# A macaron block on one core: the order in which its first pair of row blocks is fed and dequantised

## The chip, the cores and the metric

The kernel runs on one NeuronCore of a Trainium2 chip. TensorE (PE) multiplies matrices; VectorE (DVE), ScalarE (ACT) and GpSimd (POOL) do element-wise work; SyncE (SP) and, in part, ACT and POOL issue transfers (DMA). Each engine works through its own instructions in order and waits for semaphores that other engines raise. The metric is the time on the device in microseconds; three runs of the kernel before gave 862.83 to 864.76 us, with a median of 863.99.

## The reference

x is [2048, 512] in float32. The block is half a gated feed-forward net, attention, and the same net again:

```python
w = (qw[:, None, :] >> shifts[None, :, None] & MAXQ).reshape(-1, qweight.shape[1])
z = ((qz[:, :, None] >> shifts[None, None, :] & MAXQ) + 1).reshape(qzeros.shape[0], -1)
W = (w - z[g_idx]) * scales[g_idx]              # for gate, up [512, 1376] and down [1376, 512]
ffn(x) = (silu(x @ Wg) * (x @ Wu)) @ Wd
x = x + 0.5 * ffn(layernorm(x))
x = x + attention(layernorm(x))                 # one head of 128, two sequences of 1024 rows
x = x + 0.5 * ffn(layernorm(x))
```

The weights are 4-bit numbers, eight packed in an int32; each row k has a group g_idx[k] that names its row of scales and zeros.

## The kernel before

**Tiling.** The 2048 rows are four blocks of 512; a pair is two of them. The inner width 1376 is cut into NT = 11 tiles of 128 columns (the last has 96). Matrix products are made from a high and a low part of each operand (`hi` by ACT, `lo` by DVE or POOL), in three passes of fp32r. Pair 0 alone uses the plain products of this section; later pairs read weights that pair 0 has prepared, and have their own functions.

**Dequantising.** In pair 0 each weight tile is made on the fly. There are 33 units: of each tile i a gate unit, an up unit and a down unit (`unit(u)`, matrix u % 3 of tile u // 3 in the kernel before). A unit goes through these steps:
- SP loads the packed integers into one of six slots of `qs` (`load_units`, 4 transfers for gate and up, 1 for down);
- DVE unpacks them (`unpack`, L1687);
- PE multiplies a one-hot of the group indices with tables of scales and zeros (`scales_zeros`, L808 and L811: eight matmuls for gate and up, two for down), into bank Z and bank S;
- DVE subtracts the zeros (`wi`, L1603) and multiplies by the scales (`wf`, L1704), both in `dequantise`;
- ACT copies `wf` as the high part (`w_hi`, L1239), POOL subtracts for the low part (`w_lo`, L2082);
- for gate and up units, SP saves `wf` to memory (`save_full`, transfer `wfull`, L523).

`wf` has two buffers, so `wf` of unit u waits for `w_lo` and the save of unit u - 2. Banks Z and S are single, so the scales of unit u wait for `wf` of unit u - 1.

**What is needed ahead.** The scales are cut by POOL into three bf16 parts (`cut_scales`), the zeros unpacked by DVE (`unpack_zeros`), and both written with small transfers into the tables `tab_gu` and `tab_d` (`table`: three pieces of scales and one of zeros). The one-hot tables `oh_gu` and `oh_d` are made from the loaded indices `idx`. x is normalised (`ln_stats`, `ln_var`, POOL's `deviation`, `ln_shift`, `ln_apply`), transposed by PE (L1020) and split into halves (`rows_hi`, `rows_lo`).

**The order.** Each engine's order is written out by hand. `plain_top` goes over the 11 tiles for the first 512 rows: on PE gate product, up product, and down product of the tile before, with `scales_zeros` of later units between them. `keep_warm(n)` issues n multiplications of the identity, two instructions each (L736), whose results nobody reads. `plain_bottom` does the next 512 rows with the finished weights.

## Time and profile before

| what | us |
|---|---|
| median of three runs | 863.99 |
| profiled execution | 863.93 |
| its span, first to last instruction | 862.1 |
| PE busy | 833.4 (97%) |
| DVE busy | 478.3 (55%) |
| ACT busy | 270.8 (31%) |
| POOL busy | 242.5 (28%) |

The span is 1.8 us shorter than the profiled execution's time; the rest lies around it. "PEld" is the loading of weights into PE, which overlaps its work. A share is an average over stages with different limits, so the rows below take the stretches apart. In a row of the trace, L811 is line 811 of the kernel before, `ps` is the memory that PE writes, `wp` and `wd` hold the gate and up weights and the down weights, `hs` and `hT` the hidden rows. "[2.13 <-PE ps L811]" says that the engine was idle for 2.13 us ahead of the row, and what ended that.

### The profile page before, as it was taken

The page shows a single profiled execution, that of the slowest core. Times are in us where ns is not written, and L with a number is a line of the kernel's source. Part 1 is how long each engine was busy: PE and PEld are TensorE (multiplying, and loading weights), DVE is VectorE, ACT ScalarE, POOL GpSimd, SP SyncE. Part 2 cuts the span into 40 slices and gives each one's busy share as a digit, 9 for nine tenths or more (in the row PEclk, how much of TensorE's full clock was granted, in tenths as well). Part 3 has the DMA queues.
Part 4 walks back from the last instruction along what each step waited for, and adds up shares of the span by engine and source line. Part 5 has one row for each costly group of instructions (what it writes and reads, how often), then busy time and mean ns, then how long its engine had stood idle before and what let it go on. Part 6 is the DMA issues. An engine that isn't in the chain of part 4 may idle for free.

```text
span 862.1 us, 10734 instructions
## 1 busy us (share of the span) xinstructions
PE 833.4 (97%) x4040; PEld 678.7 (79%) x4040; DVE 478.3 (55%) x800; ACT 270.8 (31%) x465; POOL 242.5 (28%) x197
## 2 busy tenths in 40 slices
PE   4799999999999999999999899999999999999998
PEld 4567678887888888788888788888887888888786
DVE  5577763564745454454867677445435744434452
ACT  3233322353511211241574584112112511112121
POOL 5344331463210524030235344041510201101100
PEclk9999999999999999999999999999999999999999
DMA  5667747985485444242115126854444154444121
GB/s 130 189 209 228 232 172 233 322 327 193 167 324 170 132 162 124 74 159 75 73 62 186 46 94 254 338 170 131 163 116 167 50 195 160 142 162 141 46 97 50
DMA packets 72272, 139.36 MB, mean 162 GB/s; under 512 B 25549, under 2 KB 36477, under 8 KB 67229
## 3 DMA queue, kind: packets, MB, share of 16 engines
q1 hardware_dynamic: 70908, 136.91, 47.0%
q10 hardware_dynamic: 1152, 1.36, 0.6%
q8 instruction: 32, 0.52, 0.3%
q0 software_dynamic: 160, 0.42, 0.2%
q14 instruction: 20, 0.16, 0.1%
HBM read 100.54 MB, written 37.95 MB: 161 GB/s over the span
## 4 chain that ended last, share of the span: by engine, by line
PE 73%; DVE 2%; ACT 0%; issue 0%; POOL 0%; DVEq 0%; ACTq 0%; POOLq 0%
PE ps L722 36%; PE ps L729 33%; PE ps L740 2%; PE ps L1125 1%; DVE mx L1919 0%; DVE pT L1603 0%; DVE stats L1614 0%; POOL t L2082 0%; DVE oT L1603 0%; DVE t L1603 0%; ACT oT L1239 0%; DVE hT L1603 0%; PE ps L1051 0%; ACT pr L1463 0%; DVE u L1606 0%
## 5 line engine op out<-in xcount | busy, mean ns | idle before, releaser
L722 PE MATMUL ps<-blk,ring 128*128 128x512 f32 (+1 forms) x1386 | 320.9, 389 | 0.1
L722 PEld LDWEIGHTS ps<-blk,ring 128*128 128x128 f32 (+1 forms) x1386 | 256.7, 185 | 58.1 <-DVE blk L1603 0.5
L729 PE MATMUL ps<-wd,hT 128*128 128x512 f32 (+1 forms) x1056 | 250.8, 392 | 0.8 <-DVE hT L1603 0.7
L729 PEld LDWEIGHTS ps<-wd,hT 128*128 128x128 f32 (+1 forms) x1056 | 196.8, 188 | 43.5 <-DVE hT L1603 1.2
L2124 POOL TENSOR_TENSOR h<-h,u 128x512 f32<-128x512 f32 (+1 forms) x33 | 42.7, 1295 | 324.2 <-ACT h L1358 324.2
L729 PE MATMUL ps<-xT,wp 128*128 128x512 f32 x480 | 115.8, 396 | 0.9 <-POOL wp L2082 0.7
L729 PEld LDWEIGHTS ps<-xT,wp 128*128 128x128 f32 x480 | 88.4, 188 | 22.5 <-issue 2.0
L1606 DVE TENSOR_TENSOR u<-ps,p1s 128x512 f32<-128x512 f32 (+1 forms) x66 | 45.4, 687 | 97.3 <-PE ps L722 97.2
L1358 ACT ACTIVATE h<-h 128x512 f32<-128x512 f32 (+1 forms) x33 | 20.9, 632 | 176.1 <-DVE h L1606 176.1
L1606 DVE TENSOR_TENSOR u<-ps,u 128x512 f32<-128x512 f32 (+1 forms) x66 | 45.6, 691 | 25.6 <-PE ps L722 24.6
L1606 DVE TENSOR_TENSOR h<-ps,p1s 128x512 f32<-128x512 f32 (+1 forms) x33 | 22.8, 691 | 64.1 <-PE ps L722 64.1
L1603 DVE TENSOR_TENSOR hT<-h,hT 128x512 fp32r<-128x512 f32 (+1 forms) x44 | 30.7, 712 | 24.8 <-ACT hT L1239 24.8
L1353 ACT ACTIVATE g<-ps 128x512 f32<-128x512 f32 (+1 forms) x33 | 19.7, 598 | 76.0 <-PE ps L722 76.0
L1239 ACT ACTIVATE hT<-u 128x512 fp32r<-128x512 f32 (+1 forms) x33 | 20.9, 632 | 64.5 <-DVE u L1810 64.5
L1810 DVE TENSOR_TENSOR u<-u,g 128x512 f32<-128x512 f32 (+1 forms) x33 | 38.8, 1177 | 1.1
L2092 POOL TENSOR_SCALAR xn<-xn,mv,rstd 128x512 f32<-128x512 f32 x18 | 38.3, 2140 | 0.5
L1239 ACT ACTIVATE hT<-h 128x512 fp32r<-128x512 f32 (+1 forms) x44 | 27.0, 629 | 35.5 <-PE ps L729 35.5
L2082 POOL TENSOR_TENSOR wp<-wf,wp 128x512 fp32r<-128x512 f32 x20 | 26.6, 1332 | 38.2 <-ACT wp L1239 38.2
L1603 DVE TENSOR_TENSOR hT<-u,hT 128x512 fp32r<-128x512 f32 (+1 forms) x33 | 22.8, 692 | 23.0 <-ACT hT L1239 23.0
L2087 POOL TENSOR_TENSOR rstd<-rstd,mhalf 128x4 f32<-128x4 f32 x12 | 15.1, 1256 | 68.5 <-DVE rstd L1624 68.5
L1835 DVE SCALAR_TENSOR_TENSOR xres<-ps,xres 128x512 f32<-128x512 f32 x32 | 21.6, 689 | 18.5 <-PE ps L729 18.5
L1603 DVE TENSOR_TENSOR wi<-qs,ps 128x512 bf16<-128x512 int32 (+2 forms) x33 | 22.3, 676 | 16.0 <-PE ps L811 11.1
(124 smaller groups left out, 877.8 us busy)
## 6 DMA issues: line engine op xcount, KB each, us to landing
ring<-wsaved SPq DMA_DIRECT2D x29, 1024.0 KB, 5.0
ring<-wsaved SPq DMA_DIRECT2D x33, 768.0 KB, 4.3
wsaved<-wp SPq DMA_DIRECT2D x10, 1024.0 KB, 5.0
stream<-xres SPq DMA_DIRECT2D x32, 256.0 KB, 2.3
xn<-stream SPq DMA_DIRECT2D x8, 1024.0 KB, 7.4
xres<-stream SPq DMA_DIRECT2D x32, 256.0 KB, 3.8
...
```

The lines of the kernel that those rows point to most:

```text
L722: mm = pe.matmul(ps[0:w, bank, :], ring[:, slot, which, a, kt, 0:w], blk[:, which, b, kt, :], start=not onto and kt == 0 and n == 0, stop= ...
L729: mm = pe.matmul(bank_ap, lhs(a), rhs(b), start=first and n == 0, stop=last and n == 2)
L1239: return act.activation(dst, src, ACT.Copy)
L1353: act.activation(g1[0:w, n % 2, :], ps[0:w, product_bank(n // NT + 1, 0), :], ACT.Silu).then_inc(s_g1, 1)
L1358: act.activation(hidden(i)[0:width(i), :], hidden(i)[0:width(i), :], ACT.Silu).then_inc(s_g2, 1)
L1603: return dve.tensor_tensor(out=dst, in0=a, in1=b, op=ALU.subtract)
L1606: return dve.tensor_tensor(out=dst, in0=a, in1=b, op=ALU.add)
L1810: dve.tensor_tensor(out=u2[0:w, n % 2, :], in0=u2[0:w, n % 2, :], in1=g1[0:w, n % 2, :], op=ALU.mult)\
L1835: dve.scalar_tensor_tensor(out=xres[:, r, :], in0=ps[:, down_bank(q, half, r), :], scalar=0.5, in1=xres[:, r, :], op0=ALU.mult, op1=ALU.ad ...
L2082: return pool.tensor_tensor(out=dst, in0=a, in1=b, op=ALU.subtract)
L2092: pool.tensor_scalar(x_rows(t)[:, r, :], x_rows(t)[:, r, :], mv[:, t % 2, r, 0:1], rstd[:, t % 2, r:r + 1], ALU.subtract, ALU.mult).then_i ...
L2124: pool.tensor_tensor(out=hidden(i)[0:w, :], in0=hidden(i)[0:w, :], in1=u3[0:w, n % 2, :], op=ALU.mult).then_inc(s_h2, 1)
```

## The change

The change touches only the order and the placing of work in pair 0:
- **Units.** The order is now gate 0, up 0, gate 1, up 1, down 0, gate 2, up 2, down 1, and so on (`UNIT_ORDER`; `made(m, i)` is the place of a unit in it, counted from 1). A down unit is dequantised one tile later than before.
- **First transfers.** The down zeros are loaded first on ACT's queue (on POOL's before), the group table ahead of the gate and up zeros on SP's. POOL waits only for the scales before it cuts them, and issues the down indices behind that. The pieces of the gate and up tables are shared out between SP and ACT, and issued as they get ready.
- **Start.** PE has 6 `keep_warm` instead of 10 ahead of everything, the first unit's scales ahead of the transposes of x and the second's ahead of the last of them; 4 and 2 stand further down where 6, 6 and 6 stood. DVE unpacks the down zeros first, and does units 0 and 1 ahead of x's low halves; ACT does the high half of unit 0 ahead of x's. The one-hot of the down indices comes after tile 0's hidden rows.
- **Saves.** ACT issues the save `wfull` of a unit behind its own copy, in place of SP.
- **Second rows.** The statistics of the second 512 rows are split over two tiles, and ACT normalises them instead of DVE.
- In `scales_zeros` the matmuls for zeros and for scales alternate. ACT runs one small Silu early, so that it loads one table where it loaded two. Two semaphores of the attention weights become one.

```diff
@@ -331,8 +332,15 @@
             return e - 1 if e == NT + 2 else e - 2
+        UNIT_ORDER = ((0, 0), (1, 0)) + tuple(mi for i in range(1, NT) for mi in ((0, i), (1, i), (2, i - 1))) + ((2, NT - 1),)
         def unit(u):
-            return u % 3, u // 3
+            return UNIT_ORDER[u]
+        def made(m, i):
+            return UNIT_ORDER.index((m, i)) + 1
         def unit_view(u, flat):
             m, i = unit(u)
@@ -563,33 +567,35 @@
...
             for m in range(2):
                 sp.dma_start(sc_gu[:, m * SC:(m + 1) * SC], flat(scales[m], SC)).then_inc(d_cut_gu, 16)
+            sp.dma_start(grp[:, :], groups).then_inc(d_grp, 16)
             for m in range(2):
-                sp.dma_start(zq_gu[m * ZP:(m + 1) * ZP, :], flat(zeros[m], ZC)).then_inc(d_cut_gu, 16)
-            sp.dma_start(grp[:, :], groups).then_inc(d_grp, 16)
+                sp.dma_start(zq_gu[m * ZP:(m + 1) * ZP, :], flat(zeros[m], ZC)).then_inc(d_zq_gu, 16)
             sp.dma_start(idt[:, :], ident).then_inc(d_small, 16)
             sp.dma_start(shift[:, :], shifts).then_inc(d_small, 16)
             load_units([0])
-            sp.wait_ge(s_cut, CUT_STEPS)
-            sp.wait_ge(s_tab, ZERO_STEPS)
-            table(sp, 1)
-            load_units([1, 2])
+            for j in range(2):
+                sp.wait_ge(s_cut, 2 * j + 1)
+                for m in range(2):
+                    table(sp, m, pieces=(j,))
+            load_units([1])
+            load_units([2, 3])
             sp.wait_ge(s_cut, 2 * CUT_STEPS)
             sp.wait_ge(s_tab, 2 * ZERO_STEPS)
             table(sp, 2)
-            load_units([3, 4, 5])
+            load_units([4, 5])
             for u in range(UNITS):
-                save_full(u)
                 load_units([u + QSLOTS])
-                if u == 3:
+                if u == 5:
                     load_rows(1, x, ROWS)
...
@@ -792,22 +798,20 @@
...
-                for rows, bank in ((slice(row + Z_ROW, row + Z_ROW + g), Z_BANK), (slice(row, row + 3 * g), S_BANK)):
...
+                for k in range(1 if m == 2 else KT):
+                    for rows, bank in ((slice(row + Z_ROW, row + Z_ROW + g), Z_BANK), (slice(row, row + 3 * g), S_BANK)):
...
@@ -815,39 +819,38 @@
...
                     if i == 0:
                         plain_product(0, 0, 0, by_tile=True)
-                        scales_zeros(2)
-                        pe.wait_ge(s_wlo, 2)
+                        pe.wait_ge(s_wlo, made(1, 0))
                         plain_product(0, 0, 1, (0, 1))
                         scales_zeros(3)
                         plain_product(0, 0, 1, (2, 3))
-                        scales_zeros(4)
-                        keep_warm(6)
+                        keep_warm(2)
                         continue
                     if i == 1:
                         plain_product(0, i, 0, (0, 1))
-                        scales_zeros(5)
+                        scales_zeros(4)
                         plain_product(0, i, 0, (2, 3))
                     else:
                         plain_product(0, i, 0)
+                    scales_zeros(3 * i + 2)
+                    pe.wait_ge(s_wlo, made(1, i))
+                    plain_product(0, i, 1)
                     scales_zeros(3 * i + 3)
-                    pe.wait_ge(s_wlo, 3 * i + 2)
-                    plain_product(0, i, 1)
-                    scales_zeros(3 * i + 4)
                     if i < NT - 1:
-                        pe.wait_ge(s_wlo, 3 * i)
+                        pe.wait_ge(s_wlo, made(2, i - 1))
                         down(0, 0, i - 1)
-                        scales_zeros(3 * i + 5)
+                        scales_zeros(3 * i + 4)
...
@@ -1012,21 +1015,22 @@
...
             pe.wait_ge(d_small, 32)
-            keep_warm(10)
+            keep_warm(6)
+            pe.wait_ge(d_tab[0], 64)
+            pe.wait_ge(s_oh, 3)
+            scales_zeros(0)
             for r in range(RT):
+                if r == 3:
+                    pe.wait_ge(d_tab[1], 64)
+                    scales_zeros(1)
                 pe.wait_ge(s_ln[0], r + 1)
                 for k in range(KT):
                     mm = pe.transpose(ps[:, 4 + k, r * P:(r + 1) * P], xn0[:, 0, r, k * P:(k + 1) * P], idt[:, :])
                     if r == RT - 1:
                         mm.then_inc(s_turn, 1)
-            pe.wait_ge(d_tab[0], 64)
-            pe.wait_ge(s_oh, 3)
-            scales_zeros(0)
-            keep_warm(6)
-            pe.wait_ge(d_tab[1], 64)
-            scales_zeros(1)
-            keep_warm(6)
+            scales_zeros(2)
+            keep_warm(4)
...
@@ -1256,6 +1260,10 @@
...
                 act.wait_ge(s_wf, u + 1)
                 copy(unit_weights(u, 0), unit_view(u, wf[:, u % 2, :])).then_inc(s_whi, 1)
+                m, i = unit(u)
+                if m < 2:
+                    act.dma_start(unit_view(u, wfull[i, :, m, :]), unit_view(u, wf[:, u % 2, :])).then_inc(d_full[u % 2], 16)
...
@@ -1284,11 +1292,15 @@
...
-                    for u in (2, 3) if i == 0 else (3 * i + 3,):
-                        w_hi(u)
+                    w_hi(3 * i + 2)
+                    if i == 0:
+                        w_hi(3)
                     plain_hi(0, i)
+                    if i:
+                        w_hi(3 * i + 3)
                     w_hi(3 * i + 4)
-                    w_hi(3 * i + 5)
+                    if i in (7, 8):
+                        ln_apply(1, (0, 1) if i == 7 else (2, 3))
...
@@ -1425,17 +1436,24 @@
...
+            act.dma_start(cuts[1][4], flat(zeros[2], ZC_D)).then_inc(d_zq_d, 16)
             for r in range(RT):
                 act.dma_start(xn0[:, 0, r, :], x[r * P:(r + 1) * P, :]).then_inc(d_x0[r], 16)
             for m in range(2):
                 act.dma_start(idx[FOLD * m:FOLD * m + FOLD, GU_COLS], spread(g_idx[m])).then_inc(d_idx_gu, 16)
+            act.wait_ge(s_cst, 1)
+            act.activation(spare_act[:, :], mhalf[:, 0:1], ACT.Silu)
             act.wait_ge(s_cut, CUT_STEPS)
-            act.wait_ge(s_tab, ZERO_STEPS)
-            table(act, 0)
+            table(act, 0, pieces=(2,))
+            act.wait_ge(s_tab, 2 * ZERO_STEPS)
+            table(act, 0, pieces=(3,))
+            table(act, 1, pieces=(2, 3))
             ln_apply(0)
+            w_hi(0)
             rows_hi(0)
-            w_hi(0)
...
@@ -1713,28 +1731,34 @@
...
-                dequantise(1)
-                dve.wait_ge(s_ohd, 2)
-                one_hot(dve, hots, DOWN_COLS, 1, oh_d[:, :])
...
-                    for u in (2, 3, 4) if i == 0 else (3 * i + 3,):
-                        dequantise(u)
+                    if i != 1:
+                        dequantise(3 * i + 2)
+                    if i == 0:
+                        dequantise(3)
...
+                    plain_lo(0, i)
+                    if i == 0:
+                        dve.wait_ge(s_ohd, 2)
+                        one_hot(dve, hots, DOWN_COLS, 1, oh_d[:, :])
+                        dequantise(4)
+                        dequantise(5)
+                    else:
...
-                    plain_lo(0, i)
-                    dequantise(3 * i + 5)
...
@@ -1886,10 +1910,13 @@
...
-            dve.wait_ge(d_cut_gu, 64)
             tables = maker(dve, s_tab)
+            dve.wait_ge(d_zq_d, 16)
+            unpack_zeros(dve, tables, *cuts[1])
+            ln_stats(0, (0, 1))
+            dve.wait_ge(d_zq_gu, 32)
             unpack_zeros(dve, tables, *cuts[0])
-            ln_stats(0)
+            ln_stats(0, (2, 3))
...
@@ -1900,11 +1927,9 @@
...
-            dve.wait_ge(d_cut_d, 32)
-            unpack_zeros(dve, tables, *cuts[1])
-            dequantise(0, unpack_next=False)
+            dequantise(0)
+            dequantise(1)
             rows_lo(0)
-            unpack(1)
...
@@ -2138,24 +2163,24 @@
...
-            pool.dma_start(zq_d, flat(zeros[2], ZC_D)).then_inc(d_cut_d, 16)
-            for row, first in ((0, 0), (FOLD, D_FROM)):
-                pool.dma_start(idx[row:row + FOLD, DOWN_COLS], spread(g_idx[2][first:first + D_COLS])).then_inc(d_idx_d, 16)
             pool.memset(mhalf[:, :], -0.5).then_inc(s_cst, 1)
             pool.wait_ge(s_cst, 1)
             cutter = maker(pool, s_cut)
-            pool.wait_ge(d_cut_gu, 64)
+            pool.wait_ge(d_cut_gu, 32)
             cut_scales(pool, cutter, *cuts[0])
-            pool.wait_ge(d_cut_d, 32)
+            for row, first in ((0, 0), (FOLD, D_FROM)):
+                pool.dma_start(idx[row:row + FOLD, DOWN_COLS], spread(g_idx[2][first:first + D_COLS])).then_inc(d_idx_d, 16)
...
-            compare_low(pool, hots, DOWN_COLS, 1, oh_d[:, :])
             for u in range(UNITS):
-                if u == 16:
+                if u == 2:
+                    compare_low(pool, hots, DOWN_COLS, 1, oh_d[:, :])
+                if u == 19:
                     deviation(1)
...
```

PE from its first instruction on, before (L736 is `keep_warm`, L1020 the transposes of x, L811 and L808 `scales_zeros`, L729 products):

```order
L736 MATMUL ps<-idt 128x128 x10
L1020 MATMUL ps<-idt,xn_80 128x128 x16
L811 MATMUL ps<-tab_gu,oh_gu 128x128 x8
L736 MATMUL ps<-idt 128x128 x6
L811 MATMUL ps<-tab_gu,oh_gu 128x128 x8
L736 MATMUL ps<-idt 128x128 x6
L729 MATMUL ps<-xT_85,wp 128x512 x12
L808 MATMUL ps<-tab_d,oh_d 128x512 x2
L729 MATMUL ps<-xT_85,wp 128x512 x6
L811 MATMUL ps<-tab_gu,oh_gu 128x128 x8
L729 MATMUL ps<-xT_85,wp 128x512 x6
L811 MATMUL ps<-tab_gu,oh_gu 128x128 x8
```

and in the changed kernel (L742, L1029, L815 and L813, L735 in the same roles):

```order
L742 MATMUL ps<-idt 128x128 x6
L815 MATMUL ps<-tab_gu,oh_gu 128x128 x8
L1029 MATMUL ps<-idt,xn_81 128x128 x12
L815 MATMUL ps<-tab_gu,oh_gu 128x128 x8
L1029 MATMUL ps<-idt,xn_81 128x128 x4
L815 MATMUL ps<-tab_gu,oh_gu 128x128 x8
L742 MATMUL ps<-idt 128x128 x4
L735 MATMUL ps<-xT_86,wp 128x512 x18
L815 MATMUL ps<-tab_gu,oh_gu 128x128 x8
L735 MATMUL ps<-xT_86,wp 128x512 x6
L742 MATMUL ps<-idt 128x128 x2
L735 MATMUL ps<-xT_86,wp 128x512 x6
```

Unit 0's scales moved ahead of the transposes, unit 1's ahead of the last four, and the down block of two matmuls (L808) left the first up product.

DVE from the first `wi` on, before (L1603 with `wi` and L1704 are a unit, L1687 an unpacking, L448 the one-hot of the down indices):

```order
L1603 TENSOR_TENSOR wi<-qs,ps 128x512
L1704 TENSOR_TENSOR wf<-wi,ps 128x512
L1603 TENSOR_TENSOR xT_85<-ps,xT_85 128x512 x4
L1687 TENSOR_SCALAR qs<-qs,shift 128x512
L1603 TENSOR_TENSOR wi<-qs,ps 128x512
L1704 TENSOR_TENSOR wf<-wi,ps 128x512
L1687 TENSOR_SCALAR qs<-qs,shift 128x512
L448 SCALAR_TENSOR_TENSOR oh_d<-idf,grp,oh_d 128x768
L1603 TENSOR_TENSOR wi<-qs,ps 128x512
L1704 TENSOR_TENSOR wf<-wi,ps 128x512
L1687 TENSOR_SCALAR qs<-qs,shift 128x512
L1603 TENSOR_TENSOR wi<-qs,ps 128x512
```

and in the changed kernel (L1705 unpacking, L1621 and L1722 a unit, L1742 the hidden rows `hs`, L458 the one-hot), from the third unpacking on:

```order
L1705 TENSOR_SCALAR qs<-qs,shift 128x512
L1621 TENSOR_TENSOR xT_86<-ps,xT_86 128x512 x4
L1621 TENSOR_TENSOR wi<-qs,ps 128x512
L1722 TENSOR_TENSOR wf<-wi,ps 128x512
L1705 TENSOR_SCALAR qs<-qs,shift 128x512
L1621 TENSOR_TENSOR wi<-qs,ps 128x512
L1722 TENSOR_TENSOR wf<-wi,ps 128x512
L1705 TENSOR_SCALAR qs<-qs,shift 128x512
L1742 TENSOR_TENSOR hs<-hs,ps 128x512
L1621 TENSOR_TENSOR hT<-hs,hT 128x512
L458 SCALAR_TENSOR_TENSOR oh_d<-idf,grp,oh_d 128x768
L1621 TENSOR_TENSOR wi<-qs,ps 128x512
```

The low halves of x moved behind two whole units and three unpackings, and the one-hot from ahead of the third unit to behind the hidden rows of tile 0.

## Rows read from the trace of the kernel before

**Rows 1.** Waits of TensorE over the whole run: who waited for whom, us, times, longest.
```profile
PE ps L736 <- DMA shift<-in_shifts: 11.9, 1, 11.9
PE ps L811 <- DVE wf L1704: 6.1, 7, 1.8
```

**Rows 2.** Busy time of TensorE by stretch: length, busy, instructions, clock, DMA share, GB/s.
```profile
22.10:48.00 25.90, 19.62 (x111) 1.00 0.70 218
48.00:128.00 80.00, 79.13 (x433) 1.00 0.62 201
```

**Rows 3.** TensorE in order of time: start, length, engine, line, operation, [idle before].
```profile
11.92 4.38 PE L736 MATMUL ps<-idt 128*128 128x128 f32 x20 [11.92 <-DMA shift<-in_shifts]
...
17.98 0.41 PE L811 MATMUL ps<-tab_gu,oh_gu 4*128 4x128 bf16 x8
18.32 1.60 PE L736 MATMUL ps<-idt 128*128 128x128 f32 x12
...
22.09 3.02 PE L729 MATMUL ps<-xT,wp 128*128 128x512 f32 x12
...
26.68 1.65 PE L729 MATMUL ps<-xT,wp 128*128 128x512 f32 x6 [0.73 <-POOL wp L2082]
30.15 0.41 PE L811 MATMUL ps<-tab_gu,oh_gu 4*128 4x128 bf16 x8 [1.82 <-DVE wf L1704]
30.48 1.66 PE L729 MATMUL ps<-xT,wp 128*128 128x512 f32 x6
...
44.65 3.03 PE L729 MATMUL ps<-wd,hT 128*128 128x512 f32 x12
47.61 0.39 PE L808 MATMUL ps<-tab_d,oh_d 10*128 10x512 bf16 x2
47.93 3.04 PE L729 MATMUL ps<-xT,wp 128*128 128x512 f32 x12
```

**Rows 4.** DVE in order of time, first 45 us.
```profile
9.57 0.69 DVE L1614 BATCH_NORM_STATS2 stats<-xn 128x6 f32<-128x512 f32 x1 [0.39 <-DMA xn<-in_L_attn_x]
...
13.32 0.74 DVE L448 SCALAR_TENSOR_TENSOR oh_gu<-idf,grp,oh_gu 128x512 bf16<-128x512 f32 x1
...
18.54 0.69 DVE L1603 TENSOR_TENSOR wi<-qs,ps 128x512 bf16<-128x512 int32 x1 [2.13 <-PE ps L811]
19.27 0.69 DVE L1704 TENSOR_TENSOR wf<-wi,ps 128x512 f32<-128x512 bf16 x1
19.87 2.48 DVE L1603 TENSOR_TENSOR xT<-ps,xT 128x512 fp32r<-128x512 f32 x4
...
24.50 1.01 DVE L448 SCALAR_TENSOR_TENSOR oh_d<-idf,grp,oh_d 128x768 bf16<-128x768 f32 x1
...
29.41 0.69 DVE L1704 TENSOR_TENSOR wf<-wi,ps 128x512 f32<-128x512 bf16 x1 [2.63 <-DMA wfull<-wf]
...
43.57 0.69 DVE L1704 TENSOR_TENSOR wf<-wi,ps 128x512 f32<-128x512 bf16 x1 [3.20 <-DMA wfull<-wf]
```

**Rows 5.** SP's queue in order of time, the first save.
```profile
25.67 1.53 SPq L523 DMA_DIRECT2D wfull<-wf  x1
```

**Rows 6.** ACT in order of time.
```profile
17.76 2.06 ACT L1239 ACTIVATE xT<-ps 128x512 fp32r<-128x512 f32 x4 [1.40 <-PE ps L1020]
...
24.87 1.28 ACT L1286 ACT_TABLE_LOAD   x1
```

**Rows 7.** POOL in order of time.
```profile
15.45 2.22 POOL L445 TENSOR_SCALAR oh_d<-idf,grp 128x768 bf16<-128x768 f32 x1
20.76 1.28 POOL L2082 TENSOR_TENSOR wp<-wf,wp 128x512 fp32r<-128x512 f32 x1 [3.10 <-ACT wp L1239]
```

**Rows 8.** The saves `wfull` of the first 60 us: issue to landing.
```profile
DMA to landing us min/median/max: 2.3/3.2/6.1
```

**Rows 9.** TensorE's waits from 48 to 130 us, and DVE's normalising in order of time.
```profile
PE ps L811 <- DVE wf L1704: 0.9, 2, 0.7
...
96.37 2.90 DVE L1635 TENSOR_SCALAR xn<-xn,mv,rstd 128x512 f32<-128x512 f32 x4
```

70 lines of the change are left out of this document (35 added, 35 removed).

## The prediction

> **What bounds the kernel now.** I read the waits of TensorE first, then its busy time by stretch, then its rows in order of time, and last what the engines that feed it did. TensorE bounds the run: it is busy 833.4 of 862.1 us (the page's first part, quoted above). All that another order can win is in the 28.7 us that it idles, and in fillers that count as busy. The waits [rows 1] show two large entries: 11.9 us until the constants have landed, and 6.1 us in seven waits for DVE's product `wf`, a dequantised unit. By stretch [rows 2] TensorE is busy 19.62 of 25.90 us between 22.1 and 48.0, and 79.13 of the next 80.00. So the dequantising holds it up in the first two tiles and hardly later, and the stretch before 22.1 is a start in which nothing of the kernel's main work runs.
>
> The rows in order of time [rows 3] show where. Fillers run from 11.92 to 16.30, x's transposes follow, and unit 0's scales and zeros come only at 17.98. The first product (gate of tile 0) starts at 22.09, gate of tile 2 at 47.93. I use these two as marks: whatever the change does ahead of 47.93 is worth what it moves the second mark, since behind it TensorE is nearly full.
>
> DVE's rows [rows 4] say why. `wi` of unit 0 waits 2.13 us for TensorE's scales, because these stand behind the transposes. Then `wf` waits 2.63 us at 29.41 and 3.20 us at 43.57 for a save `wfull` to land: a buffer of `wf` is free only when the save of two units earlier has left it. The first save is issued by SP at 25.67 [rows 5], 5.7 us after its data was ready at 19.96, behind the loads that stand ahead of it in SP's queue. That is the main stall: `wf` is at 29.41, the next scales at 30.15.
>
> **Start, up to the first product.** x's statistics keep their time: DVE still waits for x's last rows until 9.57 [rows 4]. The down zeros move ahead of them; they took 1.9 us in all behind the one-hot, and now fit into time in which DVE waited for transfers. The index transfer, `nmr`, and the one-hot (ready at 13.32 + 0.74 = 14.06) move little, since their queue is the same; I take the same times. Fillers are 12 instead of 20 instructions; 20 took 4.38 us, so 12 end at 11.92 + 2.6 = 14.5. Unit 0's scales then run at 14.6 instead of 17.98, `wf` of unit 0 ends two DVE instructions of 0.69 later, near 16.5. Unit 1's scales follow at 16.5, its `wf` at 18.3. The unpacking of unit 2 (0.48) stands ahead of x's low halves, so these start at 18.8 (19.87 before), the first ending at 19.4.
>
> ACT gives the high half of unit 0 first (0.63) and then issues a save (0.6), so x's high halves start at 17.8, as before [rows 6]. POOL's low half of unit 0 (1.28 [rows 7]) ends at 18.4, not 22.04. TensorE has unit 2's scales and 8 filler instructions (12 took 1.60 us, so 1.07) from 18.35 and reaches the first product at 19.8. Bounds: 18.4, when POOL is ready and x too, and 22.09, where nothing is gained. I take 19.8: a gain of 2.3.
>
> **From the first product to gate of tile 2.** A product that is followed by a scales block lasts 2.96 us (44.65 to 47.61), a block 0.32 (47.61 to 47.93), a half product 1.6 (1.66 at 30.48, whose end overlaps what follows) [rows 3]. In the new order stand: gate 0 2.7 (nothing of another kind behind it), half 1.6, block 0.33, half 1.6, four filler instructions 0.53, half 1.6, block 0.33, half 1.6, block 0.33, up 2.96, block 0.33, down 2.96, block 0.33: 17.2 us. One wait stays. Unit 4, the first down unit, needs the one-hot of the down indices, which now stands behind tile 0's hidden rows on DVE. Up of tile 0 ends at 26.1; unpacking and `hs` end at 27.4, the ACT copy with a save ahead of it at 28.1, the low half at 28.8, the one-hot (1.01 at 24.50 [rows 4]) at 29.8. TensorE is there at 28.2 and waits about 1.5 us. Its bounds are 0 and 3, the latter if POOL's comparison (2.22 [rows 7]), which also moves between its unit copies, holds unit 2 up. So gate of tile 2 starts at 19.8 + 17.2 + 1.5 = 38.5. Before it was 47.93. One block of 0.33 has then still to be done which was done before, as the down units are now made one tile later. The gain is 47.93 - 38.5 - 0.33 = 9.1, the 2.3 of the start included.
>
> The save stalls go for this reason: ACT issues a save right behind its own copy, at about 17.2 for unit 0, and the median landing is 3.2 us [rows 8], so the buffer is free at 20.4, ahead of `wf` of unit 2 at 22. Of unit 2's and 3's saves, the same. What is late next is the chain of the down one-hot above.
>
> **Behind the mark.** Two waits of together 0.9 us for `wf` between 48 and 130 [rows 9] stood behind the statistics and x's normalising on DVE (2.90 us at 96.37 [rows 9]). That normalising goes to ACT, in two parts, and the statistics are split: I take 0.8 as gained, bounds 0 and 0.9. What covers the new ACT work: ACT is busy a third of this part (five activations of 0.6 for a tile) and gets two issues of 0.6 per tile and four activations of 0.7 once. The 22 blocks for gate and up now alternate between two rows of banks: a down block of as many columns, which alternates, takes 0.32 to the next product, a gate block 0.33 (30.15 to 30.48 [rows 3]); that is 20 x 0.01 to 0.02 = 0.3 at most, and the same as a loss if the switches cost. I take 0.1. The one table load for ACT moves ahead; the second (1.28 at 24.87 [rows 6]) lay under a wait for up of tile 0 and is worth nothing. Joining the two semaphores of the attention weights, behind a wait for pair 1's end, costs nothing.
>
> **Sum.** 9.1 + 0.8 + 0.1 = 10.0 against the profiled execution's 863.93 us (span 862.1 and 1.8 around it), which is 0.06 under the median of 863.99. That gives 854.0.
>
> **Rivals.**
> 1. *The start isn't gained, 856.0.* Index and x land later since the down zeros are issued ahead of them on ACT, and x's low halves stand behind three DVE instructions more. Of that, 20 against 12 fillers speak for a gain; against it, that x's last rows and the indices bound the start in [rows 4]. First product at 22: 2.2 less gained, 856.2 with the first unpacking late as well.
> 2. *The clock is low at the first product, 856.5.* The fillers before show both levels: 20 instructions in 4.38 us at first, 12 in 1.60 later [rows 3], that is 0.22 against 0.13 each, the 1.2 and 2.4 GHz levels, the rise coming while TensorE ran without a break from 11.92. Now there are fewer fillers, and gaps between the transposes. A first product at the lower level takes 1.6 to 2 times 3.02 us, so 1.8 to 3.0 more; I take 2.5. Against it: the idle stretch of 2 us before 30.15 did not lower the rate (six matmuls in 1.66 us behind it). The Trainium skill ("TensorE: Matmul & The Clock Gate", Part 1) says that the array runs at half rate until it has been busy for some time and falls back after idling; by this rule a thinned start could begin its main work slow. The trace has the slow start, but no fall.
> 3. *Slower: the saves set the pace, 867.5.* A save now starts a copy and an issue behind `wf`, 1.3 us. Its longest landing was 6.1 us [rows 8], at the time of x's second load. If that were the rule, `wf` of a unit would come 1.3 + 6.1 + 0.7 = 8.1 us behind that of two units earlier, where TensorE's pace for two units is 6.56. 1.5 us lost for each of nine tiles is 13.5, less the 10.0: 3.5 slower. It decides from a landing of 4.6 us on. The median of 3.2 speaks against it, and that the save no longer queues behind loads on SP. The Trainium skill ("DMA: Bandwidth & Descriptors", Queues, rings and completion order) says that each transfer engine takes the queues in turn, so that ACT's queue gets its share beside SP's; by this rule landings get shorter than 3.2. No row of before shows a save on ACT's queue.
> 4. *A shorter lead, 858.* The down units have lost a tile of lead. From a block to the low half it takes 0.41 + 0.69 + 0.69 + 0.63 + 1.29 = 3.7 us of the 6.56 that each unit now has. Were an ACT issue and a wait added to each, some tiles would wait 0.5: nine of them cost 4.
>
> **How the numbers follow.** My forecast has a chance of 0.62, own range 852 to 856. Rival 1 has 0.12, rival 2 0.12, rival 3 0.04, rival 4 0.07; 0.03 is left for a gain under 852. The range of 8 in 10 reaches from 851.8 to 857.6. A change of 0.2% (1.7 us) is what a measurement of this kernel can tell from none: faster 0.95, same 0.01, slower 0.04.
>
> **What would show it.** Right: the first product near 19.8; no wait of DVE's `wf` for a `wfull` landing; one wait of TensorE before the first down block at about 28, of 1 to 2 us, for the one-hot; gate of tile 2 near 38.5; no wait of TensorE in the nine tiles behind it. Wrong: a first product at 22 or one that takes over 4 us; saves that land over 4.6 us late again and again; waits of TensorE for `wf` or POOL's low halves in the steady tiles; or the time lost again in the later pairs, where nothing should change.

## The result and the profile after

| kernel | median us | lowest to highest | runs | ratio to before, 95% interval |
|---|---|---|---|---|
| before | 863.79 | 862.83 to 865.65 | 6 | |
| changed | 860.35 | 859.46 to 861.33 | 6 | 0.9960 [0.9948, 0.9972] |

The change is worth 3.4 us by the medians; forecast were 10.0, and 860.35 lies above the range's upper end of 857.6. The profiled execution of the changed kernel took 859.65 us, its span 857.8, so 4.3 us less than before, and the rest of this section accounts for these 4.3.

TensorE's waits (engine, line waited for, us in total, times, longest) answer to [rows 1]:

```profile
PE ps L742 <- DMA shift<-in_shifts: 7.9, 1, 7.9
PE ps L815 <- DMA tab_gu<-parts_gu: 4.0, 1, 4.0
PE ps L735 <- DVE v L1621: 3.7, 1, 3.7
PE ps L813 <- DVE oh_d L458: 1.7, 1, 1.7
...
PE ps L815 <- DVE wf L1722: 0.7, 1, 0.7
```

The seven waits for `wf` (6.1 us) are down to one of 0.7. A new one has come, 4.0 us for the table transfer `tab_gu`, and one of 1.7 for the down one-hot `oh_d`. The constants land 4 us earlier (7.9 against 11.9), the cause of which no run here takes apart, and which only lengthens the wait for the tables. In order of time (start, length, engine, line, operation, [idle before]), against [rows 3]:

```profile
7.95 2.93 PE L742 MATMUL ps<-idt 128*128 128x128 f32 x12 [7.95 <-DMA shift<-in_shifts]
14.90 0.61 PE L815 MATMUL ps<-tab_gu,oh_gu 4*128 4x128 bf16 x8 [4.03 <-DMA tab_gu<-parts_gu]
15.44 2.82 PE L1029 MATMUL ps<-idt,xn 128*128 128x128 f32 x12
...
21.62 4.36 PE L735 MATMUL ps<-xT,wp 128*128 128x512 f32 x18
...
31.39 0.39 PE L813 MATMUL ps<-tab_d,oh_d 10*128 10x512 bf16 x2 [1.66 <-DVE oh_d L458]
31.71 1.79 PE L735 MATMUL ps<-xT,wp 128*128 128x512 f32 x6
33.44 0.60 PE L815 MATMUL ps<-tab_gu,oh_gu 4*128 4x128 bf16 x8
33.97 4.19 PE L735 MATMUL ps<-xT,wp 128*128 128x512 f32 x12
...
41.68 3.06 PE L735 MATMUL ps<-xT,wp 128*128 128x512 f32 x12
```

x's transposes (L1029) take 0.23 us each here and took 0.12 before (16 of them from 16.14 to 17.98), so TensorE ran at its lower rate. The granted clock's rows show 1.00 there all the same, so in the start the rate is read off the matmuls. The first product starts at 21.62 (22.09 before), gate of tile 2 at 41.68 (47.93 before). Up of tile 1, at 33.97, takes 4.19 us where every other product of 12 matmuls in this stretch takes 3.0 to 3.1. The stretches show why (stretch, its length, PE busy, PEld, DVE, ACT, POOL, then TensorE's granted clock, DMA share, GB/s):

```profile
30.00:32.00 2.00, 0.60 (x3) 0.38 (x4) 1.41 (x3) 0.00 (x0) 0.00 (x0) 1.00 0.74 222
32.00:34.00 2.00, 2.00 (x15) 1.13 (x14) 1.70 (x3) 0.64 (x2) 0.00 (x0) 0.77 0.40 104
34.00:36.00 2.00, 2.00 (x7) 1.61 (x6) 1.77 (x3) 0.88 (x2) 1.28 (x1) 0.50 0.62 215
36.00:38.00 2.00, 2.00 (x9) 1.42 (x7) 0.00 (x0) 0.23 (x1) 1.29 (x1) 0.88 1.00 300
48.00:128.00 80.00, 80.00 (x436) 56.70 (x435) 56.29 (x100) 27.79 (x45) 33.70 (x26) 1.00 0.62 201
```

After the wait for the one-hot the granted clock fell to 0.50 (1.2 of 2.4 GHz) and was whole again before 38. From 48 on TensorE is busy all the time (79.13 of 80.00 before, [rows 2]).

Of the stall that the change was after, DVE's product `wf` waiting for a save, this is left of before's two waits of 2.63 and 3.20 us [rows 4]:

```profile
47.02 0.69 DVE L1722 TENSOR_TENSOR wf<-wi,ps 128x512 f32<-128x512 bf16 x1 [1.16 <-DMA wfull<-wf]
```

Over the whole run `DVE wf` waited for saves 7.0 us in 4 waits before, and 1.2 us in 1 after. ACT issues the first save as it starts its own copy, where SP issued it at 25.67 [rows 5], behind nine loads whose issuing had kept it from 19.89 on:

```profile
17.07 0.34 ACTq L1266 DMA_DIRECT2D wfull<-wf  x1
```

**Where the lead went.** The lead of the changed kernel over before, at the same instruction in both traces: 0.5 us at the first product, 6.25 at gate of tile 2, 6.3 at the start of pair 1 (229.49 against 235.81), 5.9 before pair 1's attention product (484.27 against 490.14), 5.0 at pair 2 (514.09 against 519.10), 5.0 at DVE's last instruction (853.85 against 858.86), 4.3 at the end of the span. The chain of waits (start, us, what) of before:

```profile
387.85 24.58 PE ps L729 x108
...
415.64 1.75 PE ps L740 x16
...
490.14 4.63 PE ps L729 x24
```

and of after:

```profile
381.56 21.84 PE ps L735 x96
...
404.90 4.51 DVE xn L1653 x4
409.46 1.97 PE ps L746 x16
...
484.27 5.49 PE ps L735 x24
```

The first loss, 0.45 us, is DVE's normalising of the attention's rows: its four instructions take 4.58 us after and 4.14 before, and they now end the chain, where TensorE's own products did. Why they take longer no run takes apart. The second, 0.86 us, is the same product in 5.49 us instead of 4.63. It stands in both kernels behind a wait of 3.6 us for `v`, and in both the clock falls behind that wait: where a later product of the same size takes 3.04 us, this one loses 1.6 us before and 2.5 after. The rows of before:

```profile
490.14 4.63 PE L729 MATMUL ps<-pT,v 128*128 128x256 f32 x24 [3.64 <-DVE v L1603]
...
502.87 3.04 PE L729 MATMUL ps<-pT,v 128*128 128x256 f32 x24
```

The granted clock of before is 1.00 from 480 to 490 and 0.83 from 490 to 500; that of after is 0.68 from 480 to 490, a stretch that holds the product from 484.27 on, and 0.98 from 490 to 500.

### The profile page after: what moved, and what is told of

Same layout as the page of the kernel before. It is cut to its first block, busy times and chain, and to the rows that moved or that the text cites. A ratio compares the mean times of both kernels' runs of the same rounds, so it can differ in the third digit from the quotient of the medians.

```text
span 857.8 us, 10671 instructions
## 1 busy us (share of the span) xinstructions
PE 833.5 (97%) x4008; PEld 678.0 (79%) x4008; DVE 477.0 (56%) x797; ACT 272.6 (32%) x469; POOL 240.9 (28%) x196
## 4 chain that ended last, share of the span: by engine, by line
PE 73%; DVE 3%; ACT 1%; issue 0%; POOL 0%; DVEq 0%; ACTq 0%; POOLq 0%
PE ps L728 37%; PE ps L735 33%; PE ps L746 2%; PE ps L1129 1%; DVE xn L1653 1%; DVE mx L1944 0%; DVE pT L1621 0%; DVE stats L1632 0%; POOL t L2107 0%; DVE oT L1621 0%; DVE t L1621 0%; ACT oT L1243 0%; DVE qT L1975 0%; DVE hT L1621 0%; ACT pr L1481 0%
## 5 line engine op out<-in xcount | busy, mean ns | idle before, releaser
L735 PE MATMUL ps<-wd,hT 128*128 128x512 f32 (+1 forms) x1056 | 251.1, 392 | 0.8 <-DVE hT L1621 0.7
L735 PEld LDWEIGHTS ps<-wd,hT 128*128 128x128 f32 (+1 forms) x1056 | 196.8, 188 | 43.7 <-DVE hT L1621 1.1
L735 PE MATMUL ps<-xT,wp 128*128 128x512 f32 x480 | 117.1, 399 | 0.0
L735 PEld LDWEIGHTS ps<-xT,wp 128*128 128x128 f32 x480 | 89.3, 190 | 21.7 <-issue 2.2
L1621 DVE TENSOR_TENSOR hT<-h,hT 128x512 fp32r<-128x512 f32 (+1 forms) x44 | 30.7, 712 | 24.8 <-ACT hT L1243 24.8
L1621 DVE TENSOR_TENSOR hT<-u,hT 128x512 fp32r<-128x512 f32 (+1 forms) x33 | 22.8, 692 | 23.1 <-ACT hT L1243 23.1
L1621 DVE TENSOR_TENSOR wi<-qs,ps 128x512 bf16<-128x512 int32 (+2 forms) x33 | 22.3, 675 | 23.1 <-PE ps L815 16.7
```

The lines of the kernel that those rows point to most:

```text
L735: mm = pe.matmul(bank_ap, lhs(a), rhs(b), start=first and n == 0, stop=last and n == 2)
L1621: return dve.tensor_tensor(out=dst, in0=a, in1=b, op=ALU.subtract)
```

## The experiments

All changes are edits of the changed kernel, except in e10. Each was timed beside the kernel before, whose median was 863.7 (a0, e1 to e3), 863.6 (e4, e5, e6, e8), 863.4 (e10 to e12) and 863.65 (e13). A run's median is of 5 executions (e3, e4, e11, e12, e13), 6 (e1, e10), 9 (e2), 11 (e6, e8) or 12 (a0, e5); its trace is of one. "Scales" is the start of the first unit's scales, "first" that of the first product, "gate 2" that of the gate of tile 2, all in the profiled execution.

| run | edit | scales | first | gate 2 | median (lowest to highest) | ratio, 95% interval |
|---|---|---|---|---|---|---|
| before | | 17.98 | 22.09 | 47.93 | 863.79 | |
| changed | | 14.90 | 21.62 | 41.68 | 860.35 (859.5 to 861.3) | 0.9960 [0.9948, 0.9972] |
| a0_again | none | 14.49 | 20.82 | 40.91 | 860.70 (857.3 to 863.4) | 0.9962 [0.9948, 0.9976] |
| e1_onehot | down one-hot earlier | 15.36 | 22.07 | 39.33 | 858.23 (855.8 to 858.9) | 0.9932 [0.9918, 0.9945] |
| e2_fill | fillers before the wait | 17.11 | 24.85 | 45.48 | 859.66 (857.5 to 862.5) | 0.9953 [0.9936, 0.9969] |
| e3_warm | more fillers at the start | 14.54 | 20.54 | 41.52 | 858.46 (857.9 to 859.9) | 0.9943 [0.9930, 0.9956] |
| e4_idx | index transfers later | 13.56 | 21.21 | 41.07 | 858.03 (857.5 to 858.7) | 0.9931 [0.9912, 0.9951] |
| e8_tabs | unit 0's load behind the tables | 16.48 | 24.21 | 45.18 | 861.10 (860.1 to 864.3) | 0.9975 [0.9962, 0.9988] |
| e5_sp | saves back on SP | 16.03 | 22.74 | 47.49 | 863.64 (861.1 to 865.8) | 0.9999 [0.9985, 1.0013] |
| e6_zs | zeros, then scales | 15.68 | 22.43 | 42.51 | 860.06 (857.1 to 862.7) | 0.9951 [0.9934, 0.9968] |
| e10_before_act | before, saves on ACT | 17.70 | 21.81 | 43.02 | 859.08 (857.2 to 860.8) | 0.9944 [0.9930, 0.9959] |
| e11_xfirst | x's transposes first | 15.24 | 21.53 | 42.04 | 859.60 (858.9 to 861.7) | 0.9958 [0.9945, 0.9970] |
| e12_four | e1, e4, e6, e11 | 14.50 | 20.91 | 39.80 | 857.10 (856.6 to 858.2) | 0.9925 [0.9913, 0.9937] |
| e13_fillers | e12 and fillers | 15.02 | 20.34 | 39.20 | 856.08 (855.8 to 856.7) | 0.9911 [0.9896, 0.9926] |

### Which part of the change is worth the time: the saves (e5, e10)

e5 takes one part of the change back:

```diff
-                    act.dma_start(unit_view(u, wfull[i, :, m, :]), unit_view(u, wf[:, u % 2, :]))...   # in w_hi
+                save_full(u)                                   # SP, ahead of load_units([u + QSLOTS])
```

> The saves of the units' dequantised weights go back from ACT's queue to SP's, ahead of the load of the same step as in the kernel before; all else stays. Theory (the saves behind SP's loads were the main stall before): DVE waits for a save to land twice again, 2 to 3 us each, gate of tile 2 comes 3 to 4 us later than 41.7 (about 45), the two short waits of TensorE in tiles 3 to 9 come back (0.9 in all), 864.5. Rival (with the first down unit made later the loads in front are gone in time, and the new order of units had done it alone): gate of tile 2 at 41.7, 860.5. If the slower pace of the tiles (9.93 us against 9.85 before) comes from saves that ACT issues, it goes back to 9.85 here.

Measured: 863.64, ratio 0.9999. Gate of tile 2 is at 47.49, only 0.44 earlier than in the kernel before. DVE's rows of e5:

```profile
27.93 0.69 DVE L1725 TENSOR_TENSOR wf<-wi,ps 128x512 f32<-128x512 bf16 x1 [3.10 <-DMA wfull<-wf]
...
32.96 0.69 DVE L1725 TENSOR_TENSOR wf<-wi,ps 128x512 f32<-128x512 bf16 x1 [3.09 <-DMA wfull<-wf]
```

The theory holds in kind; it was too mild in size (47.49, not 45), in part because TensorE's clock fell twice in this execution (0.53 from 32 to 34 and 0.50 from 38 to 40), behind waits of 1.60 and 3.12 us. Its second half fell: no wait of TensorE between 48 and 128 came back, so those 0.9 us weren't the saves'. The pace of the tiles stayed as in the changed kernel (see e6), so ACT's issuing isn't its cause either.

e10 makes the same edit alone in the kernel before (and lets SP wait for the last saves before it loads over their buffer, after the last tile).

```diff
-                save_full(u)
...
+                    act.dma_start(unit_view(u, wfull[i, :, m, :]), unit_view(u, wf[:, u % 2, :]))...   # in w_hi
```

> The kernel before with one edit of the change alone: ACT issues the saves of the dequantised units behind its own copy, SP no longer does. Theory (the place of the saves is what the change's gain comes from; with the saves back on SP the changed kernel took as long as the kernel before): DVE's waits of 2.63 and 3.20 us for a save are gone, gate of tile 2 comes near 43.5 instead of 47.93, the time is 860.5 or less. Rival (the saves pay only together with the new order of units and the new start): other waits take their place, gate of tile 2 at 46 or later, 862 to 863.7.

Measured: 859.08, ratio 0.9944. The one edit gives all that the whole change gives, and gate of tile 2 comes at 43.02, near the theory's 43.5. No wait of DVE's `wf` for a save is left; the short waits in TensorE's rows are others:

```profile
26.40 1.67 PE L730 MATMUL ps<-xT,wp 128*128 128x512 f32 x6 [0.73 <-POOL wp L2086]
...
36.14 0.40 PE L812 MATMUL ps<-tab_gu,oh_gu 4*128 4x128 bf16 x8 [0.56 <-DVE wf L1708]
```

The two waits of 0.9 us between 48 and 128 are there again, as before, since this kernel still normalises x's second rows on DVE.

```profile
PE ps L812 <- DVE wf L1708: 0.9, 2, 0.7
```

e5 and e10 together: with the saves on SP the rest of the change is worth nothing that can be measured; with the saves on ACT it adds nothing. What helps is the time of issue, not a quicker landing: in the first 60 us the median from issue to landing is 3.2 us before, 3.3 after and 3.9 in e10.

### The wait for the down one-hot, and the clock behind it (a0, e1, e2, e3)

> The changed kernel itself, unaltered, for a second trace and time beside the others. 860.4 us by every theory. What it tells apart is what of the changed kernel's trace repeats: if the lower clock after the wait for the one-hot (up product of tile 1 in 4.2 instead of 3.0 us) and the slow transposes (x12 in 2.8 us) belong to the order, they are there again; if they are chance, they are not. The same for the 0.9 us by which the later attention stretch was slower, and the 0.7 us more behind the last TensorE instruction.

The unaltered kernel again: 860.70, between 857.3 and 863.4 in twelve executions. Up of tile 1 is slow again (4.02 us, the granted clock 0.53 and 0.62 from 32 to 36), after a wait of 1.65 us. The slow transposes (2.64 for 12), the product of 5.49 us in pair 1's attention and the longer end of the span (4.0 us behind DVE's last instruction) are there again too.

e1 makes the one-hot between units 2 and 3 on DVE:

```diff
                     if i == 0:
+                        dve.wait_ge(s_ohd, 2)
+                        one_hot(dve, hots, DOWN_COLS, 1, oh_d[:, :])
                         dequantise(3)
...
                     if i == 0:
-                        dve.wait_ge(s_ohd, 2)
-                        one_hot(dve, hots, DOWN_COLS, 1, oh_d[:, :])
                         dequantise(4)
```

> The one-hot of the down indices goes on DVE from behind tile 0's hidden rows to between units 2 and 3, where DVE idled 1.6 us. Theory A (the wait of 1.7 us for it lowers TensorE's clock as well): the wait is gone, the clock stays high, up product of tile 1 takes 3.0 instead of 4.2 us, gate of tile 2 starts at 38.5 instead of 41.7, time 857.2. Theory B (only the wait costs, the clock falls for another reason): the product stays at 4.2, time 858.7. Theory C (DVE's next unit is late instead): no gain, 860.4.

Measured: 858.23. Theory A fits: its 857.2 left out that the first product came 0.45 us later here than in the changed kernel. The interval of e1 lies just clear of that of the unaltered a0. In TensorE's rows of e1 the wait is gone and up of tile 1 has its full rate:

```profile
30.12 0.39 PE L813 MATMUL ps<-tab_d,oh_d 10*128 10x512 bf16 x2
30.44 1.66 PE L735 MATMUL ps<-xT,wp 128*128 128x512 f32 x6
32.41 0.40 PE L815 MATMUL ps<-tab_gu,oh_gu 4*128 4x128 bf16 x8 [0.30 <-DVE wf L1722]
32.73 3.03 PE L735 MATMUL ps<-xT,wp 128*128 128x512 f32 x12
```

From the first product to gate of tile 2 it took 17.26 us, 20.06 in the changed kernel: 2.80, of which 1.36 is the wait (1.66 less the 0.30 left) and 1.4 the clock. e2 leaves the wait and puts 12 filler matmuls ahead of it (`pe.matmul` of the identity into a bank that nobody uses then):

> Six filler multiplications (twelve instructions) into an unused bank ahead of the block that waits for the one-hot, nothing else. Theory A (idling TensorE there lowers its clock): the up product of tile 1 is back at 3.0 us though the block starts at the same 31.4, gate of tile 2 starts 1.4 earlier at 40.3, time 859.0. Theory B (the clock falls whatever TensorE does there): nothing changes, 860.4, or 0.2 more for fillers that overrun.

Measured: 859.66, too near the unaltered kernel's 860.70 for the times to decide. 0.33 us of idle time is left, and up of tile 1 takes 3.03: the clock stayed up. One execution is weak evidence for that, since two with the whole wait (e4 and e11, below) kept it up too; but of the four executions with 0.20 to 0.65 us of idle time near this place (e1, e2, e12, e13) none fell, and of the seven with 1.65 to 1.70 us five did. This execution had its tables late (17.11) and its first product at the lower rate (6.30 us for 18 matmuls), and lost more in the start than the edit won. e3 puts 36 fillers where 12 stood at the start (`keep_warm(18)` for `keep_warm(6)`):

> 18 instead of 6 fillers at the very start, so that TensorE works from 7.95 until about 14.3 instead of idling from 10.9 to 14.9. Theory A (that idle time is why scales and transposes run at the low clock): the 16 transposes take 2.0 instead of 3.8 us, the scales blocks 0.4 instead of 0.6, and the first product starts at 20.4 instead of 21.6: 859.2. Theory B (the start is bound by DVE and ACT behind the tables, TensorE's clock is hidden there): first product within 0.3 of 21.6, 860.4.

Measured: 858.46, with the first product at 20.54, as theory A said. But a0, whose scales came as early (14.49), had it at 20.82, so the fillers gave 0.3 us there at most, and the product then took 5.26 us. TensorE ran without a break from 8.62 to 14.6, and x's transposes took 1.53 us for 12 where they had taken 2.82; but the 1.66 us wait, ahead of 31.21, and the slow up of tile 1 (3.98) were there as before.

### The start (e4, e8, e11)

The changed kernel's first scales wait for the tables. e4 lets POOL issue the two transfers of the down units' indices later:

```diff
-            for row, first in ((0, 0), (FOLD, D_FROM)):
-                pool.dma_start(idx[row:row + FOLD, DOWN_COLS], ...)
             pool.wait_ge(d_cut_d, 16)
             cut_scales(pool, cutter, *cuts[1])
             deviation(0)
+            for row, first in ((0, 0), (FOLD, D_FROM)):
+                pool.dma_start(idx[row:row + FOLD, DOWN_COLS], ...)
...
-            pool.wait_ge(d_idx_d, 32)
-            clamp(pool, hots, DOWN_COLS, GD)
             for u in range(UNITS):
+                if u == 1:
+                    pool.wait_ge(d_idx_d, 32)
+                    clamp(pool, hots, DOWN_COLS, GD)
```

POOL's own work on these indices (`clamp`) moves behind unit 0's low half with them.

> POOL issues the two transfers of the down units' indices behind the gate and up tables' deviation instead of ahead of it. What is asked: why unit 0's scales wait until 14.90 us for the table transfers, which the prediction left out. Theory (the index transfers, many small packets, share the DMA engines with the tables between 10 and 13 us): the first scales run at 13.5 or earlier, the first product at 20.2 to 20.6, and the time is 859.3, 1.2 less than the changed kernel's 860.5. The one-hot of the down units isn't delayed, since it waits for other work until 31. Rival (the tables' own packets take that long): first scales at 14.5 to 15.4 as before, 860.5.

Measured: 858.03, 2.5 us less than the changed kernel, more than expected, and with a spread of 1.3 us in five executions, where the unaltered kernel a0 had 6 in twelve. (The intervals of the two still overlap.) The tables land earlier:

```profile
13.56 0.60 PE L815 MATMUL ps<-tab_gu,oh_gu 4*128 4x128 bf16 x8 [2.42 <-DMA tab_gu<-parts_gu]
...
21.21 5.52 PE L735 MATMUL ps<-xT,wp 128*128 128x512 f32 x18
```

In the profiled execution the first product took 5.52 us for 18 matmuls, 4.36 in the changed kernel, as the clock was low then (0.58 and 0.56 from 20 to 24): the 1.3 us won at the scales weren't kept there. After the same wait for the one-hot (1.67 us) the clock did not fall here. The scales started between 14.49 and 17.11 us in the six profiled executions with the changed kernel's start (changed, a0, e1, e2, e5, e6; e3 at 14.54, where fillers stood before them); this spread of 2.6 us is part of that of the times. The 13.56 of e4 is one draw as well, 0.9 us below the earliest of six. That the index transfers hold the tables up is made likely by it and by the median, not shown; e12 and e13, which hold them back too, have x's transposes ahead of the scales and can't tell.

e8 puts unit 0's large load behind the first table pieces on SP:

> SP issues unit 0's weight load behind the first four table pieces instead of ahead of them. Theory (the big load fills the DMA engines until about 10 us and pushes the small table transfers behind it): first scales at 13.0 to 14.0, first product up to 1 us earlier, 859.7, unless unit 0's weights then come last. Rival (the tables are late because of their own sources and packets, so the place in the queue is nothing): first scales at 14.5 to 15.4, 860.5.

Measured: 861.10, with the scales at 16.48, although SP issued its table pieces 2.5 us earlier, from 4.20 us on. No gain shows in the trace or the time, so nothing here speaks for the load as what keeps the tables.

e11 puts x's transposes ahead of the scales again:

```diff
-            pe.wait_ge(d_tab[0], 64)
-            pe.wait_ge(s_oh, 3)
-            scales_zeros(0)
             for r in range(RT):
-                if r == 3:
-                    pe.wait_ge(d_tab[1], 64)
-                    scales_zeros(1)
                 ...transposes...
+            pe.wait_ge(d_tab[0], 64)
+            pe.wait_ge(s_oh, 3)
+            scales_zeros(0)
+            pe.wait_ge(d_tab[1], 64)
+            scales_zeros(1)
             scales_zeros(2)
```

> The changed kernel with x's 16 transposes ahead of the first unit's scales again; scales of units 0, 1 and 2 follow one another. Theory (the scales wait for the tables until 14.9 while ACT has x's rows normalised from 11.6 to 13.8, so this part of the change put work that was ready behind work that wasn't): TensorE does the transposes within the wait, unit 1's scales come 1.1 us earlier, the first product at 20.0 to 20.6 instead of 21.62, in line with where the tables land, and 859.3. Rival (the first product waits for x's low halves on DVE and for POOL, both behind the tables): 21.6 and 860.5.

Measured: 859.60 and the first product at 21.53, so neither fits wholly: the transposes did run within the wait (11.69 to 15.3), but the fillers and the gate that follow ran at the low clock (0.50 from 20 to 24), behind two waits of 1.67 and 1.57 us:

```profile
17.30 0.40 PE L815 MATMUL ps<-tab_gu,oh_gu 4*128 4x128 bf16 x8 [1.67 <-DVE wf L1721]
19.27 0.60 PE L815 MATMUL ps<-tab_gu,oh_gu 4*128 4x128 bf16 x8 [1.57 <-DVE wf L1721]
19.81 2.07 PE L742 MATMUL ps<-idt 128*128 128x128 f32 x8
21.53 6.14 PE L735 MATMUL ps<-xT,wp 128*128 128x512 f32 x18
```

Against the unaltered kernel's 860.70 its 859.60 can't be told apart.

### The blocks of zeros and scales (e6)

```diff
-                for k in range(1 if m == 2 else KT):
-                    for rows, bank in (...Z_BANK...), (...S_BANK...):
+                for rows, bank in (...Z_BANK...), (...S_BANK...):
+                    for k in range(1 if m == 2 else KT):
```

> The zeros' and the scales' matmuls of a gate or up unit run in two blocks, one for each row of banks, as before, instead of in turn. Theory (alternating between the banks slows the product beside them): the pace of a tile goes from 9.93 back to 9.85 us, 0.8 in the nine tiles of pair 0, 859.7. Rival (the slower pace has another cause, as the saves on ACT's queue): 9.93 stays, 860.5.

Measured: 860.06, too near 860.70 for the times to decide. The traces do: from gate of tile 2 to the transposes of x's second rows it is 85.49 us before (0.87 of it waits), 85.46 in the changed kernel and 85.45 in e5, both without waits, and 84.92 in e6. The other traces agree: the three with two blocks and no wait (e6, e12, e13) have 84.91 to 84.92, the eight that alternate without a wait 85.45 to 85.46. The alternation between the banks costs 0.54 us here; the product ahead of such a block is 2.95 us long in the order of before and 2.98 in the other, as these rows of e6 (first) and of the changed kernel show (start to start):

```profile
45.49 0.41 PE L815 MATMUL ps<-tab_gu,oh_gu 4*128 4x128 bf16 x8
45.83 3.01 PE L735 MATMUL ps<-xT,wp 128*128 128x512 f32 x12
48.77 0.41 PE L815 MATMUL ps<-tab_gu,oh_gu 4*128 4x128 bf16 x8
```

```profile
44.67 0.40 PE L815 MATMUL ps<-tab_gu,oh_gu 4*128 4x128 bf16 x8
45.00 3.06 PE L735 MATMUL ps<-xT,wp 128*128 128x512 f32 x12
47.98 0.39 PE L815 MATMUL ps<-tab_gu,oh_gu 4*128 4x128 bf16 x8
```

### A faster kernel (e12, e13)

e12 is the changed kernel with the edits of e1, e4, e6 and e11.

> The changed kernel with four edits: x's transposes ahead of the scales, the down units' index transfers behind the deviation on POOL, the down one-hot on DVE between units 2 and 3, and the zeros and scales in two blocks. If what each took apart adds up: start 1.2 (e11) and 1.3 (index transfers), one-hot 2.8 at gate of tile 2, blocks 0.5: first product at 19.3, gate of tile 2 at 36.5, 855.0. If the gains share one cause (a higher clock in the start) or a new wait stands in the way, 857 to 858, as the best of them alone.

Measured: 857.10, the second of the two cases. Gate of tile 2 at 39.80, not 36.5: the start was at the low clock once more (gate of tile 0 in 6.14 us), as in e11. e13 adds fillers where TensorE waits:

```diff
             scales_zeros(0)
+            keep_warm(5)
             pe.wait_ge(d_tab[1], 64)
             scales_zeros(1)
+            keep_warm(5)
             scales_zeros(2)
```

> The kernel with four edits (e12) and 10 filler matmuls behind each of the first two units' scales, where TensorE waited 1.69 and 1.63 us for wf; before had 12 in each of these places. Theory (e12 missed its 855.0 because TensorE's clock fell over these two waits, so that the gate of tile 0 took 6.14 us where 4.5 is its time at full rate): the gate of tile 0 takes 4.4 to 4.6, gate of tile 2 comes at 38.0 to 38.4 instead of 39.80, and the time is 855.4. Rival (the clock is low there for another reason, as the long stretch of filler and transposes at low rate from 8 us on): 6.1 us again and 857.1.

Measured: 856.08 (855.8 to 856.7), ratio 0.9911 [0.9896, 0.9926]: the lowest median of the study, 4.3 us under the changed kernel's. Its interval lies clear of e10's, so the rest of the change, with these edits, is worth something beside the saves; it overlaps that of e12. The gate of tile 0 ran at full rate:

```profile
20.34 3.01 PE L735 MATMUL ps<-xT,wp 128*128 128x512 f32 x12
23.51 1.66 PE L735 MATMUL ps<-xT,wp 128*128 128x512 f32 x6 [0.16 <-POOL wp L2108]
```

Its granted clock in the start against e12's, which stands first:

```profile
22.00:24.00 2.00, 2.00 (x6) 1.56 (x5) 1.27 (x2) 0.00 (x0) 2.00 (x2) 0.50 0.48 159
```

```profile
22.00:24.00 2.00, 1.84 (x8) 1.20 (x7) 1.70 (x3) 0.61 (x2) 1.92 (x3) 1.00 0.49 155
```

The theory on the clock holds in this execution, against e11 and e12, where the clock fell here both times. Gate of tile 2 came at 39.20 instead of 38.4: with the clock up, TensorE meets the next limit, short waits for POOL's low halves (0.16 and 0.53 us) and for `wf` (0.65).

## Why the prediction was wrong

The direction was right, the size wasn't: 4.3 us in the profiled executions instead of 10.0. The terms of the sum, against the traces of before and after:

| step of the prediction | forecast | measured | difference |
|---|---|---|---|
| "A gain of 2.3" in the start | 2.3 | 0.47 | 1.8 |
| first product to gate of tile 2, "17.2" and a wait of "1.5" | 18.7 | 20.06 | 1.4 |
| behind the mark, "0.8" and "0.1" (less the block of 0.33) | 0.57 | 0.03 | 0.5 |
| later pairs, "where nothing should change" | 0 | -0.45 and -0.86 | 1.3 |
| after DVE's last instruction | 0 | -0.7 | 0.7 |

The differences add up to the 5.7 us that are missing. The largest is the start: the step that failed there is its missing term for the table transfers. The second is the clock behind the wait for the one-hot, which the sum put at nothing.

**The start: failed.** "Unit 0's scales then run at 14.6" was near for the wrong reason: 14.90. The prediction had the scales wait for the fillers; in the trace they wait for the table transfers, for which the sum had no term at all. TensorE idled 4.03 us ahead of them and did x's transposes behind them at the low clock (2.82 us for 12). "x's statistics keep their time" and "I take the same times" were wrong in the kernel's favour: the one-hot ended near 11.5 instead of 14.06 and the normalising began at 10.89, so x was ready before the scales; the new order put ready work behind late work. That the first product gained 0.47 us in this execution is itself one draw: in the six executions with the changed kernel's start it came at 20.82 to 24.85, at 22.4 in the mean, no earlier than in before (22.09) and e10 (21.81). Rival 1 ("the start isn't gained") is what happened there, by another mechanism than it named.

**The wait for the one-hot: right.** Forecast "about 28 ... waits about 1.5 us", and found at 29.7 with 1.66, the 1.8 us later start included. The products of this stretch were right too: e1, in which the wait is all but gone, takes 17.26 us for the forecast's 17.2.

**The clock behind the wait: failed.** The prediction read from [rows 3] that "the idle stretch of 2 us before 30.15 did not lower the rate", and concluded that "the trace has the slow start, but no fall"; so the sum had no term for it. The reading of that stretch is right, the conclusion isn't: before's own trace has a fall in pair 1's attention (4.63 us for 3.04, above). In the changed kernel a wait of 1.66 us was followed by 1.4 us of loss at the low level (from the product behind the wait to gate of tile 2 it took 9.97 us, 8.59 in e1 without its wait of 0.30; a0, e3, e6 and e8 lose the same 1.4). It happened behind five of seven such waits of 1.65 to 1.70 us (changed, a0, e3, e6, e8; not in e4 and e11). So one wait without a fall bounds nothing. The Trainium skill ("TensorE: Matmul & The Clock Gate", Part 1) says that the array falls back to half rate after idling. By that rule the trace agrees, and the prediction gave it too little weight; what it doesn't tell is that the same wait has a fall behind it in one execution and none in another. Rival 2 put the low clock at the first product. In the changed kernel that product ran at the full rate (18 matmuls in 4.36 us, the granted clock 1.00 from 20 to 30), so rival 2 isn't what happened in it; but e2, e3, e4, e8, e11 and e12 have it there (5.22 to 6.30 us), in e11 and e12 with 1.5 us more for gate of tile 0 than in e13.

**The saves: right, and they were the whole gain.** Both waits of [rows 4] are gone, because ACT issued the first save at 17.07, as forecast ("about 17.2"). Rival 3 had expected shorter landings from ACT's queue; they did not get shorter: the median of the first 60 us is 3.3 us, before 3.2 [rows 8], and the longest 6.7, before 6.1. The prediction treated them as one of several parts; e10 shows that one line of the change carries it. Rival 3 (the saves set the pace) left one wait of 1.16 us on DVE that TensorE did not wait for.

**Behind the mark: half right.** The two waits for `wf` went, by moving the normalising, as forecast (they stayed in e10 and were absent in e5). The alternating blocks, booked as a gain of 0.1, cost 0.54; the bound for a loss had been 0.3. Rival 4 (a shorter lead) did not happen: TensorE waits nowhere from 48 to 128.

**Later pairs: not foreseen.** "Behind it TensorE is nearly full" holds for pair 0 only. In pair 1's attention DVE's chain is near the critical path, and 0.45 of the lead ends there. 0.86 is the clock behind a wait of 3.6 us that both kernels have. In six of the fourteen profiled executions (changed, a0, e3, e6, e8, e10) the product behind it took 5.49 us, in the other eight, of kernels with and without the change, 4.3 to 4.6: it is a draw, not the change. The five of the six that have the change are the same five whose clock fell behind the wait for the one-hot, so the losses of 1.4 and 0.9 us came together; why, no run shows.

**What stays open.** After DVE's last instruction starts, the span goes on for 3.2 to 3.3 us in the two kernels with before's program (before, e10) and for 3.9 to 4.0 in all with the change's. No row names what ends it, and no run took it apart.
